# Mixer phase: two sums moved onto TensorE's identity matmuls, sigmoid by tanh, table loads issued ahead, and a new slot order

## What is computed

```
x = x + 0.5 * _L1_ffn_ref(_layernorm(x), gate_w, gate_b, expert_w, expert_b)
x = x + _L1_attn_ref(_layernorm(x), W_in, A_log, dt_bias, B_norm_bias, C_norm_bias, W_out)

# _L1_ffn_ref: 8 experts, weighted with how often each is in the top two
expert_out = relu(einsum('bsd,ehd->bseh', x, expert_w) + expert_b)
out = einsum('bseh,e->bsh', expert_out, counts) / total

# _L1_attn_ref: a selective state space layer, 32 heads of 8, state 64, R = 2
dt = clip(softplus(dt_raw + dt_bias), 0.0001, 0.5)
lam = sigmoid(lam_raw)
xg = (lam * dt)[..., None, None] * xh
xb = ((1.0 - lam) * dt * alpha)[..., None, None] * x_prev
...
y = (y_intra + y_inter).reshape(B, T, D_INNER)
y = _rms(y * silu(z))
return y @ W_out
```

## Time and profile before

| | |
|---|---|
| median of three runs | 2701.39 us (2700.14 to 2702.03) |
| the profiled execution | 2698.95 us |
| its span, first to last instruction | 2697.2 us |
| mixer phase within the span | about 1640 to 2555 us |
| busy share over the span | PE 81%, DVE 71%, ACT 55%, POOL 55% |
| mean granted TensorE clock, share of full speed | 0.908 |

### The profile page before, as it was taken

How to read it: one execution, slowest core, us unless ns; L and a number is a source line. 1 busy time by engine, 2 the same in 40 slices (tenths; PEclk the granted TensorE clock), 3 DMA queues, 4 the chain that set the end, 5 groups by cost and what they waited for, 6 DMA issues and landing times. The chain is left out here.

```text
span 2697.2 us, 38247 instructions
## 1 busy us (share of the span) xinstructions
PE 2181.0 (81%) x12996; PEld 947.5 (35%) x12996; DVE 1910.3 (71%) x4700; ACT 1478.3 (55%) x2794; POOL 1491.9 (55%) x1344
## 2 busy tenths in 40 slices
PE   2689988988898899899889864678778777877477
PEld 1223323332332333233233222444444444444343
DVE  5777777777677677767777522677888788786487
ACT  2166566656656665665666553446556555654155
POOL 3365665656566556656656431365566556655266
PEclk8799999999999999999999976788989898997599
DMA  2212112111211211121112001000000000000021
GB/s 109 51 46 56 32 30 50 36 44 34 54 36 26 50 40 40 38 50 36 26 46 47 6 9 44 4 13 13 9 9 17 9 9 13 13 5 5 20 67 47
DMA packets 73281, 86.81 MB, mean 32 GB/s; under 512 B 9216, under 2 KB 59520, under 8 KB 72960
## 3 DMA queue, kind: packets, MB, share of 16 engines
q1 hardware_dynamic: 73088, 84.37, 12.5%
HBM read 21.16 MB, written 12.58 MB: 13 GB/s over the span
## 5 line engine op out<-in xcount | busy, mean ns | idle before, releaser
L320 DVE TENSOR_REDUCE mS<-ps 128x1 f32<-128x512 f32 x1024 | 677.2, 681 | 304.0 <-PE ps L655 299.3
L452 ACT ACTIVATE pr<-ps 128x512 f32<-128x512 f32 x1024 | 585.7, 597 | 392.8 <-PE ps L639 373.5
L518 POOL TENSOR_TENSOR prs<-pr 128x512 f32<-128x512 f32 x384 | 487.2, 1288 | 248.9 <-ACT pr L452 248.9
L639 PE MATMUL ps<-qst,kst 97*128 97x512 f16 x1024 | 398.5, 392 | 52.7 <-ACT pr L452 51.5
L655 PE MATMUL ps<-kst,qst 96*128 96x512 f16 x1024 | 402.4, 394 | 34.1 <-DVE mS L320 23.3
L677 PE MATMUL ps<-pr,vt 128*32 128x512 f32 x2048 | 282.1, 624 | 0.0
L639 PEld LDWEIGHTS ps<-qst,kst 97*128 97x128 f16 x1024 | 99.2, 98 | 422.2 <-ACT pr L452 306.2
L522 POOL TENSOR_TENSOR terms<-terms 128x512 f32<-128x512 f32 x128 | 162.4, 1269 | 89.2 <-DVE terms L313 89.2
L313 DVE TENSOR_TENSOR terms<-ps,rope 128x512 f32<-128x512 f32 x256 | 173.2, 679 | 34.8 <-POOL lo L527 28.8
L527 POOL TENSOR_TENSOR lo<-terms,hi 128x512 f16<-128x512 f32 x128 | 148.0, 1157 | 76.9 <-ACT hi L432 76.9
L655 PEld LDWEIGHTS ps<-kst,qst 96*128 96x128 f16 x1024 | 101.3, 99 | 147.2 <-DVE mS L320 76.6
(11 more groups left out here) (266 smaller groups left out, 4434.5 us busy)
## 6 DMA issues: line engine op xcount, KB each, us to landing
qst<-hi SPq DMA_DIRECT2D x128, 128.0 KB, 2.4
kst<-hi SPq DMA_DIRECT2D x128, 128.0 KB, 2.4
qst<-lo SPq DMA_DIRECT2D x64, 128.0 KB, 2.4
kst<-lo SPq DMA_DIRECT2D x64, 128.0 KB, 2.4
x<-in_q SPq DMA_DIRECT2D x16, 256.0 KB, 2.9
rope<-in_rope SPq DMA_DIRECT2D x1, 4096.0 KB, 12.8
x<-yold SPq DMA_DIRECT2D x16, 256.0 KB, 2.5
m_x<-x SPq DMA_DIRECT2D x16, 256.0 KB, 2.8
```

The costliest lines, as they stand in the source:

```text
L320: v.tensor_reduce(mS[:, b % 2, t, s:s + 1], ps[:, 2 + n % 2, :], AX, ALU.max).then_inc(S["s_read"], 1)
L452: a.activation(pr[:, s % 2, g, :], ps[:, g % 2, :], ACT.Exp, scale=ATT_SCALE).then_inc(S["exp"], 1)
L518: g.tensor_tensor(prs[:, c, :], pr[:, 0, c, :], pr[:, 1, c, :], ALU.add).then_inc(S["prs"], 1)
L639: mm(ps[:, g % 2, :], kst[:, h, P * kt:P * kt + P], qst[:, h, :], start=True, stop=True).then_inc(S["st"], 1)
```

## The change

Five edits, all of them in the mixer phase and its loading of weights:

1. The last two of the three additions over experts (`rl[0] + rl[2]` on POOL, `acc + rl` on DVE) are gone. PE now sums the three parts while it turns them: each 128 x 128 block is three matmuls against the identity which accumulate in PSUM, where one transpose stood.
2. The same for a chunk's output: the addition of the halves of `pt` (DVE) and that of `own` (POOL, `whole_output`) are gone, and `turn_y` is three accumulating matmuls a block.
3. `lam`'s sigmoid is written as half of one plus the hyperbolic tangent of half the argument. ACT's exp of `lam` becomes a tanh issued with the gates; DVE's addition, reciprocal and multiplication become one `scalar_tensor_tensor`, and the factor of two that is left is taken back in `bc_bias`.
4. ACT's function tables are loaded by explicit instructions ahead of the wait for the data. One load an iteration is gone, since sine, silu and tanh now stand under one table.
5. `nmean` is computed by POOL in place of DVE, and `MIXER_AT` has new numbers.

```diff
@@ steps (DVE)
-                    wait(v.tensor_scalar(lam[:, :, :], lam[:, :, :], 1.0, None, ALU.add))
+                    m = mark(v.scalar_tensor_tensor(gam, lam[:, :, :], 1.0, dt[:, :, :], ALU.add, ALU.mult))
+                    dve.wait_ge(S["dve"], n)
...
-                    wait(v.reciprocal(lam[:, :, :], lam[:, :, :]))
-                    wait(v.tensor_tensor(gam, lam[:, :, :], dt[:, :, :], ALU.mult))
-                    v.tensor_tensor(bet[:, :, :], dt[:, :, :], gam, ALU.subtract).then_inc(S["beta"], 1)
+                    dve.wait_ge(S["dve"], m)
+                    v.scalar_tensor_tensor(bet[:, :, :], dt[:, :, :], 2.0, gam, ALU.mult, ALU.subtract).then_inc(S["beta"], 1)
@@ products (DVE)
-                    dve.wait_ge(S["prod"], upto("prod", b, t + 1))
-                    v.tensor_tensor(pt[:, t % 2, 0], pt[:, t % 2, 0], pt[:, t % 2, 1], ALU.add).then_inc(S["pair"], 1)
@@ deviations (POOL), and gone from statistics (DVE)
+                    g.tensor_scalar(nmean[:, k, :], mv[:, k, :, 0], -1.0, None, ALU.mult)
@@ gates, soft, decays (ACT)
+                    if b:
+                        act.wait_ge(S["beta"], all_of("beta", b - 1))
+                    act.wait_ge(S["ev_b"], all_of("ev_b", b))
+                    a.activation(lam[:, :, :], lam_raw, ACT.Tanh, scale=0.5)
+                    a.preload_act_table_set("exp_and_others")
...
-                    a.activation(lam[:, :, :], lam_raw, ACT.Exp, scale=-1.0)
                     a.activation(dt[:, :, :], t_dt[:, :, :], ACT.Exp).then_inc(S["act"], 1)
+                    a.preload_act_table_set("natural_log")
...
+                    a.preload_act_table_set("exp_and_others")
...
+                    a.preload_act_table_set("silu_and_others")
                     act.wait_ge(S["ang"], all_of("ang", b))
@@ own_token (ACT)
-                        act.wait_ge(S["y_sum"], upto("y_sum", b, t - 1))
+                        act.wait_ge(S["yT"], upto("yT", b, t - 1))
@@ turn_y (PE)
-                    pe.wait_ge(S["y_sum"], upto("y_sum", b, t + 1))
+                    pe.wait_ge(S["prod"], upto("prod", b, t + 1))
+                    pe.wait_ge(S["own_w"], upto("own_w", b, t + 1))
...
-                        ins = nc.tensor.transpose(ps[:, 5, P * c:P * c + P], pt[:, t % 2, 0, P * c:P * c + P],
-                                                  w["ident"][:, :])
+                        for k, part in enumerate((own[:, t % 2, 0], pt[:, t % 2, 0], pt[:, t % 2, 1])):
+                            ins = mm(ps[:, 5, P * c:P * c + P], part[:, P * c:P * c + P], w["ident"][:, :],
+                                     start=k == 0, stop=k == 2)
@@ sumT (PE)
-                                pe.wait_ge(S["summed"], all_of("summed", ffn))
+                                pe.wait_ge(S["added"], all_of("added", ffn))
+                                pe.wait_ge(S["ex_v"], all_of("ex_v", ffn))
                                 for t in range(NT):
...
+                                    for k, part in enumerate((acc[:, 1], rl[:, 0], rl[:, 2])):
+                                        ins = mm(ps[:, 2, P * t:P * t + P], part[:, P * t:P * t + P], w["ident"][:, :],
+                                                 start=k == 0, stop=k == 2)
@@ MIXER_AT, two of its rows
-    "own": (0, 1, 13, 19), "own_p": (1, 5, 11, 25), "whole": (5, 8, 18, 39), "turn_y": (7, 10, 19, 27),
-    "gated": (7, 11, 18, 35), "squares": (9, 13, 25, 28), "mean": (10, 15, 25, 33), "mean_read": 40, "stats": 0,
+    "own": (1, 2, 21, 27), "own_p": (0, 5, 10, 35), "turn_y": (11, 18, 35, 41),
+    "gated": (12, 22, 36, 47), "squares": (15, 22, 37, 40), "mean": (18, 31, 40, 44), "mean_read": 50, "stats": 1,
```

More of the change, by code:

```diff
@@ L969 @@
 MIXER_AT = {
-    "wo": 1, "out": 1, "stats_gate": 2, "xn_gate": 5, "turn_gate": 6, "gate": 7, "top": 8, "variants": (0, 5, 11, 12),
-    "chunks": (2, 7, 16, 20), "states": (2, 6, 14, 19), "chunks_rest": (5, 9, 19, 22), "products": (5, 9, 18, 28),
-    "own": (0, 1, 13, 19), "own_p": (1, 5, 11, 25), "whole": (5, 8, 18, 39), "turn_y": (7, 10, 19, 27),
-    "gated": (7, 11, 18, 35), "squares": (9, 13, 25, 28), "mean": (10, 15, 25, 33), "mean_read": 40, "stats": 0,
[L975 to L978, removed]
+    "wo": 3, "out": 4, "stats_gate": 4, "xn_gate": 5, "turn_gate": 10, "gate": 11, "top": 11,
+    "variants": (0, 9, 14, 21), "chunks": (4, 11, 26, 34), "states": (7, 10, 29, 34), "chunks_rest": (9, 11, 32, 39),
+    "products": (9, 12, 30, 42), "own": (1, 2, 21, 27), "own_p": (0, 5, 10, 35), "turn_y": (11, 18, 35, 41),
+    "gated": (12, 22, 36, 47), "squares": (15, 22, 37, 40), "mean": (18, 31, 40, 44), "mean_read": 50, "stats": 1,
+    "xn": 4, "turn": 5, "experts": (10, 12, 13, 17, 19, 22, 29, 30), "sumT": 33, "y": 34, "stats2": 39, "xn2": 39,
+    "turn2": 42, "project": (2, 3, 4, 8), "gates": 10, "shift": 9, "soft": 10, "steps": 13, "norm_bc": 7, "sums": 21,
+    "angles": 26, "weights": 27, "rotate": 30, "diagonal": 44, "diagonal_p": 31, "bt": 35, "scores": 39, "mask": 46,
 }
@@ L1037, in mixer_phase @@
         PER = {"var": 2, "shift": 2, "xn": 2, "xT": 2, "xnT": 2, "ex": EXPERTS,
-               "relu": EXPERTS // 2, "ex_v": EXPERTS // 2, "added": EXPERTS // 2 - 1, "summed": 1, "sumT": 1, "y": 1, "var2": 1, "shift2": 1, "xn2": 1, "xT2": 1, "xnT2": 1,
+               "relu": EXPERTS // 2, "ex_v": EXPERTS // 2, "added": EXPERTS // 4, "sumT": 1, "y": 1, "var2": 1, "shift2": 1, "xn2": 1, "xT2": 1, "xnT2": 1,
                "gate": 1, "gate_read": 1, "wo": 1, "y2": 1,
@@ L1115, in expert @@
                     ins.then_inc(S["ex_v"], 1)
[L1117 to L1120, removed]
                 def shift_dt(b):
@@ L1514, in _ @@
                                 own_term(scan, AT["own_p"].index(q))
-                            if q in AT["whole"]:
-                                whole_output(scan, AT["whole"].index(q))
                         if ffn is not None and q in AT["experts"] and AT["experts"].index(q) % 4 == 3:
```

21 lines of the change are left out of this document (4 added, 17 removed).

## The result

The changed kernel takes 2627.02 us in the median of 4 runs (2624.34 to 2629.81), the kernel before 2700.93 (2700.14 to 2702.03): a ratio of 0.9729, interval 0.9716 to 0.9743. The profiled execution took 2626.98 us, with a span of 2625.2.

What follows compares the result with a forecast made beforehand. An iteration was bound by PE's work, 40.5 us, plus its waits, 11.1. Work 40.5 - 3.0 + 6.9 = 44.4 plus waits 3.2 gave 47.6; thirteen iterations -52, edges -1.5: 2701.4 - 53.5 = 2648 us, range 2612 to 2688.

Steps and rivals of the forecast that it cites:

- PE's new work: turn_y and the experts' sum as accumulating matmuls, 1.46 and 2.93 us each: together +6.9 us of PE work per full iteration.
- PE's waits: In each full mixer iteration, PE's waits for other engines fall from 11.1 to 3.2 us.
- The clock: In each iteration's half-clock stretch, the clock stays up and gives back 3.0 us of PE work (bounds 0 and 3.5).
- rival D: Clock still falls between chunk_rest of chunks 2 and 3: +1.0 us per iteration, 2715 us or above; chance 0.10.
- The distance: Time between residuals of neighbouring batches: 47.6 us, 4.0 less than 51.56; thirteen full iterations give -52.
- B: PE's busy time overstated by modelled group tails, waits about 1 us: 6.2 us less per iteration, 2619 us; chance 0.17.
- the edges: First and last mixer iterations: iteration 0 +1.8, iteration 17 +2.7, iterations 1, 2 and 16 -6; together -1.5 us.
- A: The forecast itself: PE bounds the iteration at full clock with some 3 us of waits; 2630 to 2665 us, chance 0.50.
- The Trainium skill's rule: PE's weight loading, 46% of the iterations, would leave half its time to spare, so the +6.9 us costs nothing.
- C: New order waits elsewhere, DVE behind longer PE matmuls: 2 us taken back, 49.6 us an iteration, 2674 us; chance 0.15.

Runs made afterwards that it cites:

- e10: The changed kernel plus idle identity matmuls on PE, three and five, in its waits for chunk 1's and chunk 2's states: 2612.72 us, ratio 0.9676.
- e12: The changed kernel with `weights` in slot 29, the last `own` in slot 31, and three idle matmuls at each of two state waits: 2597.23 us, ratio 0.9619.
- e9: The changed kernel with DVE's third `gated` moved from slot 36 to 30, ahead of its `turn_y`: 2682.88 us, ratio 0.9939.
- e5: The changed kernel with lambda's sigmoid by exponential and reciprocal again, as in the kernel before: 2673.44 us, ratio 0.9908.
- e6: The changed kernel without explicit table loads, each load behind its activation's wait, five an iteration: 2677.18 us, ratio 0.992.
- e3: The changed kernel with only turn_y's sum undone, so DVE and POOL add the three parts again: 2831.53 us, ratio 1.0492.
- e8: As e3, with the third `own_p` moved from slot 10 to 13, behind POOL's whole_output of chunk 1: 2732.29 us, ratio 1.0116.
- e11: The changed kernel with lambda's old sigmoid (exponential and reciprocal) and three and eight idle matmuls in PE's two state waits: 2655.22 us, ratio 0.9824.
- e7: The changed kernel with `weights` moved from slot 27 to 29: 2624.83 us, ratio 0.9723.
- e1: All of the changed kernel's new code with the slot numbers of the kernel before: 2695.32 us, ratio 0.9985.
- e4: The changed kernel with only the experts' sum undone, DVE's addition at slot 31 and POOL's second addition back: 2726.95 us, ratio 1.0102.
- e2: The code of the kernel before in the new slot order, with slots added for its two old pieces: 2881.5 us, ratio 1.0683.

## Why the prediction was right, and what it had wrong

**PE's new work** was right: a turn_y 1.44 us (1.46 forecast), the experts' sum 2.9 at full clock (1745.06 to 1747.94), PE's work 43.97 us an iteration (44.4). That the total came so near is in part luck. Where the clock stays up PE is busy 42.83 us (1749.70 to 1796.40), so that at full clock 4.6 us of the old 40.5 were given back where I took 3.0 and at most 3.5, and the falls that are left take 1.1 of them again.

**PE's waits** were right in sum, 3.9 against 3.2: states 2.57 (2.5), POOL's sum 0.37 (0.6), squares 0.33 (0.3). I missed 0.63 for ACT's `m_xn`, which was 0.24 before.

**The clock** came back, but not all of it: 0.97 in the iterations, where I asked for more than 0.97, and 0.5 for 3.4 us in nine of twelve. That was my sign for rival D. It is there with a small part of D's price: 47.87 - 46.70, 1.2 us an iteration, where D had 5. The place is not D's either: seven of the nine falls begin at the wait of 1.08 us for chunk 1's states, two behind the 1.49 for chunk 2's with the experts' 0.36. I had read from one iteration of before that waits up to 2 us are harmless; e10 shows that these are not, and other iterations of before's own trace could have told me. At 2133 us the clock falls for 3.4 us behind a wait of 0.92, some 3 us after it had come up:

```profile
2132.91 0.61 PE L1657 MATMUL m_ps<-m_ones,m_sqy 128*128 128x2 f32 x4 [0.92 <-ACT m_sqy L1397]
```

**The distance** of 47.87 against 47.6 is right to 0.3 us; twelve intervals and the one ahead of them gave 49.5 where thirteen should give 52. DVE's work came to 38.0 us (36.1 forecast), POOL's to 28.4 (27.5), ACT's to 27.3. What I had counted did go; but pieces that now stand beside other work became longer, POOL's two steps on `m_own` from 5.6 to 8.1 us an iteration. One sum was off: the range's lower end, B's time less the edge bound, is 2610 and not 2612.

**The step that was mis-sized is the edges**: -1.5, between -10 and +8, forecast; -21.0 measured in start and drain. That is 19.5 of the 21 us by which the time was missed. The rest is small: 2.5 too much for the thirteen iterations, 1.5 elsewhere in the span, and the 2.4 by which before's median lay above its profiled execution, which the changed kernel does not show. I priced them by half-clock passes (24 x 0.226 us and 12 x 0.226 us), as if the clock there stayed where it was. It rose from 0.73 to 0.85 in the start and from 0.64 to 0.76 in the drain. The sum had two terms, and both were off by about 10 us. PE's work should have grown by 12.6 and grew by 3.3 (77.45 to 78.99 and 77.22 to 78.97). Chains and waits should have given 14.2 (2.8, 5.4 and 6) and PE's idle time fell by 24.3 (47.35 to 32.71 and 46.88 to 37.23). In the start, the wait for the experts' sum of batch 1, before:

```profile
1706.90 1.12 PE L1711 MATMUL m_ps<-ident,m_acc 128*128 128x128 f32 x4 [7.71 <-DVE m_acc L1120]
```

and after:

```profile
1700.76 0.49 PE L1707 MATMUL m_ps<-ident,m_acc 128*128 128x128 f32 x2 [3.79 <-POOL m_rl L1491]
```

Iteration 0, for which I had added 1.8, did not change; batch 1 gave 3.8 us and batch 2 9.1, where I took 2 for each. What the risen clock and what the shorter waits are worth by themselves at the edges is read from the windows; no run changed the edges alone.

**Rivals.** The time, 2627, is nearer to B's 2619 than to A's, but not for B's reason. B (PE's busy time overstated, its waits down to about 1 us) asked for 45.4 us an iteration and fell: the distance is 47.87 with 3.9 us of waits, and even e12, at full clock and with those waits shortened or filled, takes 45.9. The Trainium skill's rule that I had set on B's side (Perfetto Trace Analysis, Identifying the Most-Contended Engine) judges PE's room by the share of weight loading, beside a rate of operations that no row here gives. That share is 360.41 of 574.4 us, 63%. This trace does not bear out that the rest of PE's time was free: `L1701` above runs its six 512-column passes end to end in 2.93 us, 0.49 each, four times the 0.12 of a 128-column pass, and weight loading is busy for only 1.22 of these 2.92 us. C did not come in the kernel as it stands, but the order was as dangerous as C says: e9's one slot costs 56 us.

**A sentence that was wrong without showing in the number:** that the savings of DVE and ACT count for nothing where PE did not wait for them. Exponential and reciprocal again cost 46 us (e5), the loads behind their waits, with one more of them, 50 (e6). The sum came out because I took these parts as given and only counted PE's waits in the whole. Nor do the parts add up. Undone one at a time from the changed kernel, they cost 68 (order), 204 or 105 (turn_y's sum), 100 (experts' sum), 46 and 50 us, for 74 us together; `nmean` alone was never put back. Where a sum was undone its pieces got slots by guess, and e3 against e8 shows that one slot of such a guess can be half of the price. So 105 and 100 are the price of taking a piece away under this order, not what it is worth under its own best one. That each slot is fitted to the lengths that all edits together make is how I read this: what is late in one queue delays the next, until PE waits and its clock falls.

## What to carry to other kernels

When an engine in order is given longer or shorter work, list what stands behind each consumer of its results in that consumer's queue: there a slot number is worth more than the instruction saved. Test such a change whole, and its parts by taking one away, not by their sum. Where the fullest engine is TensorE, look for half clock behind the short waits too, over all iterations of the trace and not in one: here 3.4 us of it followed a wait of 1.08, and a few idle matmuls in such waits paid for themselves.

## What the runs showed of the hardware that was not expected

**Of two elementwise engines side by side, the one that starts second takes longer.** POOL's two steps on `m_own`, after, the first pair beside DVE's large multiply, the second not (timeline of POOL, after, and the two multiplies of DVE at the same place):

```profile
2162.30 1.87 POOL L1496 TENSOR_TENSOR m_own<-m_own 128x256 f32<-128x256 f32 x1 [4.43 <-ACT m_own L1376]
2164.25 2.15 POOL L1497 TENSOR_TENSOR m_own<-m_own,m_dec 128x256 f32<-128x256 f32 x1
...
2178.68 0.73 POOL L1496 TENSOR_TENSOR m_own<-m_own 128x256 f32<-128x256 f32 x1
2179.49 0.63 POOL L1497 TENSOR_TENSOR m_own<-m_own,m_dec 128x256 f32<-128x256 f32 x1
...
2161.83 1.75 DVE L1193 TENSOR_TENSOR m_xv<-m_xr,m_coef 128x1536 f32<-128x1536 f32 x1
2164.16 1.75 DVE L1193 TENSOR_TENSOR m_xv<-m_xr,m_coef 128x1536 f32<-128x1536 f32 x1
```

Each POOL step ends 0.5 to 0.6 us after the multiply that started ahead of it, a little less than its own length alone, and the multiply keeps its 1.75. In e11 it is the other way round: POOL's addition starts 0.11 us ahead and takes 1.32, the multiply `m_xv` beside it 2.82, and 1.74 a little later. It looks as if the second did most of its work only when the first had ended. No run isolated this; it is read from the overlaps.

**The iterations' lengths come in clusters.** Means over twelve iterations: 45.9 and 46.7 (e12, e10); 47.65 and 47.87 (e7, after); 49.5 (e11); 51.0, 51.0, 51.2, 51.6 and 51.8 (e9, e6, e5, before, e1); 54.6 and 54.8 (e4, e8); then 61.4 and 64.9 (e3, e2). Some of this nearness is of means only: e9 has iterations of 50.8 and 52.4, e8 of 53.2 to 57.4, and e1's execution is the one 10 us above its median. But e5 and e6, changes as different as a sigmoid and the table loads, have ten of twelve iterations each within 0.1 us of 51.2, and the kernel before has seven there. In the changed kernel eight of the last twelve iterations are within 0.02 us of 46.69 or 48.26, the other four 47.4 to 47.5 and 49.0. That the clock steps between two levels fits this; why just these lengths stays open.
